# Row normalisation and softmax division moved from VectorE to GpSimd, and the expert product moved one step back in the plan

## What is computed

```
x = x + attn_a(layernorm(x))    # 16 heads of 8, softmax over all keys, mask after the softmax
x = x + ffn(layernorm(x))       # 8 routed experts, top 2 of each row, and one shared expert
x = x + attn_b(layernorm(x))    # rotary q and k, no mask, w_out and a bias behind it
x = x + ffn(layernorm(x))       # the same weights again
layernorm(x) = (x - mean) / sqrt(var + 1e-5)
swiglu(x)    = (silu(x @ w1) * (x @ w3)) @ w2
```

## Time and profile before

| | |
|---|---|
| median of 3 runs | 1904.55 us (1900.91 to 1908.56) |
| the profiled execution | 1906.13 us, its span 1904.1 us |
| mean granted TensorE clock | 0.976 |
| PE busy | 97% |
| DVE busy | 82% |
| ACT busy | 75% |
| POOL busy | 46% |

### The profile page before, as it was taken

One profiled execution on the slowest core, in us unless ns is written; L12 is line 12 of the kernel. 1 busy time (PEld: TensorE's weight loads), 2 busy tenths in 40 slices (PEclk: granted clock), 3 DMA queues, 4 the chain that ended last, 5 costly groups with the idle time before them and its releaser, 6 DMA issues.

```text
span 1904.1 us, 44343 instructions
## 1 busy us (share of the span) xinstructions
PE 1852.5 (97%) x16816; PEld 885.6 (47%) x16816; DVE 1566.8 (82%) x3083; ACT 1432.9 (75%) x2840; POOL 883.0 (46%) x1210
## 2 busy tenths in 40 slices
PE   6999999999999999999999999999999999999997
PEld 3444444444444444444444444444444444444446
DVE  4988998888888888988889888988888888788826
ACT  3388887777777777777788787778877877777782
POOL 6142333455655567555643434435334454544520
PEclk8599998999999999999999999999999999999999
DMA  7111110000100101001100101001100010000000
GB/s 254 35 68 68 58 42 3 1 28 27 52 2 35 35 24 47 2 35 35 35 35 2 51 25 62 2 2 52 40 19 8 2 30 29 24 2 8 7 2 12
DMA packets 39380, 61.91 MB, mean 33 GB/s; under 512 B 5632, under 2 KB 20608, under 8 KB 39040
## 3 DMA queue, kind: packets, MB, share of 16 engines
q1 hardware_dynamic: 39168, 59.08, 9.5%
HBM read 30.74 MB, written 27.26 MB: 30 GB/s over the span
## 4 chain that ended last, share of the span: by engine, by line
PE 86%; DVE 9%; ACT 2%; issue 2%; POOL 1%; DMA 0%; DVEq 0%; ACTq 0%; POOLq 0%
PE ps_sum L1212 28%; PE ps_banks L1178 20%; PE ps_banks L1232 11%; PE ps_banks L1153 9%; PE ps_banks L1253 8%; DVE negmax L940 5%; PE ps_banks L1124 2%; PE ps_banks L1167 2%; PE ps_banks L1131 1%; DVE xn L958 1%; PE ps_banks L1110 1%; PE ps_banks L1223 1%; ACT sums L810 1%; PE ps_banks L1138 1%; PE ps_banks L1160 1%
## 5 line engine op out<-in xcount | busy, mean ns | idle before, releaser
L940 DVE TENSOR_REDUCE negmax<-ps_banks 128x1 f32<-128x512 f32 x2048 | 1280.7, 680 | 196.0 <-PE ps_banks L1153 192.4
L803 ACT ACTIVATE probs<-ps_banks 128x512 f32<-128x512 f32 x2048 | 1085.7, 604 | 195.2 <-PE ps_banks L1178 182.5
L1153 PE MATMUL ps_banks<-kx,qx 24*128 24x512 f32 x2048 | 650.0, 507 | 7.4 <-DVE hid L991 3.6
L1178 PE MATMUL ps_banks<-qx,kx 26*128 26x512 f32 x2048 | 528.6, 500 | 3.5 <-DVE hid L991 1.8
L1212 PE MATMUL ps_sum<-probs,vg 128*9 128x256 f32 (+1 forms) x6144 | 463.8, 374 | 6.8 <-ACT sums L810 6.0
L1178 PEld LDWEIGHTS ps_banks<-qx,kx 26*128 26x128 f32 x2048 | 197.3, 183 | 374.1 <-issue 168.1
L692 POOL TENSOR_SCALAR scaled<-scaled,gates 128x128 f32<-128x128 f32 x516 | 182.9, 372 | 283.1 <-ACT scaled L854 244.2
L1153 PEld LDWEIGHTS ps_banks<-kx,qx 24*128 24x128 f32 x2048 | 260.4, 185 | 103.6 <-ACT probs L803 55.1
L664 POOL TENSOR_TENSOR pdiag<-probs,causal 128x512 f32<-128x512 f32 x128 | 163.5, 1278 | 173.3 <-ACT probs L803 172.4
L680 POOL TENSOR_TENSOR hid<-hid,first 128x512 f32<-128x512 f32 x129 | 164.9, 1278 | 125.8 <-DVE hid L991 121.4
L1212 PE MATMUL ps_sum<-probs,w 128*9 128x256 f32 (+1 forms) x2560 | 187.7, 365 | 2.0 <-ACT sums L810 1.3
(11 more groups left out here) (104 smaller groups left out, 1289.0 us busy)
## 6 DMA issues: line engine op xcount, KB each, us to landing
qk_rows<-limbs SPq DMA_DIRECT2D x36, 512.0 KB, 3.5
qx<-qk_rows SPq DMA_DIRECT2D x128, 96.0 KB
kx<-qk_rows SPq DMA_DIRECT2D x128, 96.0 KB
qx<-mlimbs SPq DMA_DIRECT2D x512, 2.0 KB
qk_rows<-prod_c SPq DMA_DIRECT2D x8, 512.0 KB, 3.7
qk_rows<-prod_s SPq DMA_DIRECT2D x4, 512.0 KB, 2.7
out_dram<-x SPq DMA_DIRECT2D x8, 256.0 KB, 2.3
x<-in_x SPq DMA_DIRECT2D x3, 512.0 KB, 5.9
```

The costliest lines, as they stand in the source:

```text
L803: act.activation(m.probs[:, blk % PROB_SLOTS, EXP_HEADS[k], :], bank, ACT.Exp, scale=SCALE).then_inc(s.freed[SCALAR], 1)
L940: dve.tensor_reduce(m.negmax[:, unit // UNITS % 2, half, col:col + 1], bank, AX.X, ALU.max, negate=True).then_inc(s.freed[VECTOR], 1)
L1153: pe.matmul(bank_of(("scores", unit, k)), m.qx[rows, n % SLOTS, tile * P:(tile + 1) * P], m.kx[rows, n % SLOTS, half * CHUNK:(half + 1) * ...
L1178: pe.matmul(bank, m.kx[rows, n % SLOTS, j * P:(j + 1) * P], m.qx[rows, n % SLOTS, half * CHUNK:(half + 1) * CHUNK], start=True, stop=True) ...
```

## The change

- `apply` runs on POOL. It adds the negated mean and multiplies by the deviation. `deviations` on POOL gets one more small instruction that negates the means (`lower`), and the copy of the means on DVE goes. `apply` stands 3 steps behind `stats` everywhere, where it stood 4 or 5.
- The division is on POOL, in `finish`, together with the addition to x. The reciprocal stays on DVE. Both stand two steps behind `sums`.
- `gated_hidden` runs on DVE at a new item `product`, one step behind `h3`; `hidden` on POOL stays in the step where it was.
- Reads of the ring are counted by a new order, `freed`, in which `h3` counts where `product` stands.
- The expert layers start 2 steps later, and the items behind the second attention 3 steps later.

```
+H3_AT = 3
 def projected_a(c, at):
-    return staged(at, (0, ("stats", 0, c)), (1, ("moments", 0, c)), (4, ("apply", 0, c)), (6, ("turn", 0, c)),
+    return staged(at, (0, ("stats", 0, c)), (1, ("moments", 0, c)), (3, ("apply", 0, c)), (6, ("turn", 0, c)),
...
 def feed_forward(k, at):
-    return staged(at, (0, ("h1", k)), (3, ("h3", k)), (4, ("hidden", k)), (7, ("y", k)), (9, ("gate", k)))
+    return staged(at, (0, ("h1", k)), (H3_AT, ("h3", k)), (H3_AT + 1, ("product", k)), (H3_AT + 1, ("hidden", k)),
+                  (7, ("y", k)), (9, ("gate", k)))
...
-        more, at = routed(1, b * HALVES, HALVES, (b + 1) * HALVES * of_chunk + 11)
+        more, at = routed(1, b * HALVES, HALVES, (b + 1) * HALVES * of_chunk + 13)
...
-        at = (CHUNKS + c + 1) * of_chunk + 9
+        at = (CHUNKS + c + 1) * of_chunk + 12
...
-        add_side(side, {(p + 1) * UNITS + 2 * WEIGH_LAG + 3: [("sums", p)]})
+        add_side(side, staged((p + 1) * UNITS + 2 * WEIGH_LAG + 3, (0, ("sums", p)), (2, ("finish", p))))
...
+        self.read = {SCALAR: {}, VECTOR: {}}
+        for item in plan:
+            held = ("h3", *item[1:]) if item[0] == "product" else item
+            if held[0] in READER and item[0] != "h3":
+                read = self.read[READER[held[0]]]
+                read[held] = len(read)
...
 def deviations(layer, c):
-        pool.wait_ge(s.stats_kept, i + 1)
+        pool.wait_ge(s.stats_done, (i + 1) * CT)
...
+        pool.tensor_scalar(m.lower[:, i % 2, :], m.mv[:, i % 2, :, 0], -1.0, 0.0, ALU.mult, ALU.add
+                           ).then_inc(s.shifted, 1)
...
+    def apply(layer, c):
+        n, i = counts.nth("apply", layer, c), counts.nth("stats", layer, c)
+        pool.wait_ge(s.rstd_done, i + 1)
+        if n >= 2:
+            turned = [item for item in counts.turns if item[0] == "turn"][n - 2]
+            pool.wait_ge(s.filled[SCALAR], counts.use(*turned) + 1)
+        for t in range(CT):
+            tile = c * CT + t
+            last = pool.tensor_scalar(m.xn[:, n % 2, t * P:(t + 1) * P], m.x[:, tile_cols(tile)],
+                                      m.lower[:, i % 2, t:t + 1], m.rstd[:, tile:tile + 1], ALU.add, ALU.mult)
+        last.then_inc(s.xn_done, 1)
...
+    def finish(p):
+        src = m.sums[:, p % 2 * CHUNK:(p % 2 + 1) * CHUNK].rearrange("p (t h r) -> p t h r", t=CT, h=GH)
+        pool.wait_ge(s.inverted, p + 1)
+        pool.tensor_tensor(dst, src[:, :, :, 0:HD], m.recip[:, turn, :, :].to_broadcast([P, CT, GH, HD]), ALU.mult
+                           ).then_inc(s.finished, 1)
+        if masked_after(n):
+            pool.tensor_tensor(cols, cols, dst.rearrange("p t h d -> p t (h d)"), ALU.add).then_inc(s.headed, 1)
...
+    def invert(p):
+        dve.wait_ge(s.freed[SCALAR], counts.freed("sums", p) + 1)
+        if p >= 2:
+            dve.wait_ge(s.finished, p - 1)
+        dve.reciprocal(m.recip[:, turn, :, :], src[:, :, :, HD:HD + 1]).then_inc(s.inverted, 1)
...
-            pe.wait_ge(s.freed[READER[holder[0]]], counts.use(*holder) + 1)
+            pe.wait_ge(s.freed[READER[holder[0]]], counts.freed(*holder) + 1)
```

More of the change, by code:

```diff
@@ L266, in ended @@
     items = [("weigh", blk, part) for blk in range(last - WEIGH_LAG, last) for part in range(2)]
-    items += [("copy", p), ("sums", p)]
+    items += [("copy", p), ("sums", p), ("finish", p)]
     units = list(range(done, 2 * LAYER_UNITS))
@@ L275, in ended @@
         add_side(side, {1 + i * (late - 1) // len(stages): stage})
-    items += [("h1", done), ("h3", done)]
+    items += [("h1", done), ("h3", done), ("product", done)]
     for i, k in enumerate(units):
@@ L279, in ended @@
         if i + 1 < len(units):
-            items += [("h1", k + 1), ("h3", k + 1)]
+            items += [("h1", k + 1), ("h3", k + 1), ("product", k + 1)]
         items.append(("mix", k))
@@ L332, in use, with freed @@
         return self.uses[READER[item[0]]][item]
+    def freed(self, *item):
+        return self.read[READER[item[0]]][item]
     def bank(self, *item):
@@ L629, in low_of_x @@
         t = counts.turns[("turn", layer, c)]
-        pool.wait_ge(s.freed[SCALAR], counts.use("turn", layer, c) + 1)
+        pool.wait_ge(s.freed[SCALAR], counts.freed("turn", layer, c) + 1)
         pool.tensor_tensor(m.x_lo[:, slot, :], m.xt[:, t % 2, :], m.x_hi[:, slot, :].bitcast(F32),
@@ L648, in split_max @@
     def split_max(p):
-        pool.wait_ge(s.freed[SCALAR], counts.use("maxima", p) + 1)
+        pool.wait_ge(s.freed[SCALAR], counts.freed("maxima", p) + 1)
         if p:
@@ L700, in add_scaled @@
         x = m.x[:, chunk_cols(c)]
-        pool.wait_ge(s.freed[SCALAR], counts.use(*item) + 1)
+        pool.wait_ge(s.freed[SCALAR], counts.freed(*item) + 1)
         if i:
@@ L732, in pool_program @@
             mask(*of)
-        elif kind == "sums" and masked_after(place(*of)[0]):
-            add_heads(*of)
+        elif kind == "apply":
+            apply(*of)
+        elif kind == "finish":
+            finish(*of)
         elif kind == "hidden":
@@ L948, in combine @@
                           ).then_inc(s.combined, 1)
[L950 to L958, removed]
-                                     m.mean[:, tile:tile + 1], m.rstd[:, tile:tile + 1], ALU.subtract, ALU.mult)
-        last.then_inc(s.xn_done, 1)
-    def finish(p):
-        n, half = place(p)
-        _, b, g = group_of(n)
+    def invert(p):
         turn = slice(p % 2 * CT, (p % 2 + 1) * CT)
-        dve.wait_ge(s.freed[SCALAR], counts.use("sums", p) + 1)
+        dve.wait_ge(s.freed[SCALAR], counts.freed("sums", p) + 1)
+        if p >= 2:
+            dve.wait_ge(s.finished, p - 1)
         src = m.sums[:, p % 2 * CHUNK:(p % 2 + 1) * CHUNK].rearrange("p (t h r) -> p t h r", t=CT, h=GH)
         dve.reciprocal(m.recip[:, turn, :, :], src[:, :, :, HD:HD + 1]).then_inc(s.inverted, 1)
-        dve.wait_ge(s.inverted, p + 1)
-        if masked_after(n):
-            if p >= 2:
-                dve.wait_ge(s.headed, p - 1)
-            dst = m.heads[:, turn, :, :]
-        else:
-            c = b * HALVES + half
-            if c >= 2:
-                dve.wait_ge(s.filled[SCALAR], counts.use("oturn", c - 2) + 1)
-            dst = m.attn[:, c % 2, :].rearrange("p (t n h d) -> p t n h d", t=CT, n=NG, h=GH)[:, :, g, :, :]
-        dve.tensor_tensor(dst, src[:, :, :, 0:HD], m.recip[:, turn, :, :].to_broadcast([P, CT, GH, HD]), ALU.mult
-                          ).then_inc(s.finished, 1)
     def gated_hidden(k):
@@ L1028, in chain @@
             last = ("logits", layer, c + width - 1)
-            dve.wait_ge(s.freed[SCALAR], counts.use(*last) + 1)
+            dve.wait_ge(s.freed[SCALAR], counts.freed(*last) + 1)
         if k == 2:
@@ L1086, in vector_program @@
             combine(*of)
-        elif kind == "sums":
-            finish(*of)
-        elif kind == "h3":
+        elif kind == "finish":
+            invert(*of)
+        elif kind == "product":
             gated_hidden(*of)
@@ L1121, in queries_keys @@
         t = counts.turns[("turn", layer, c)]
-        pe.wait_ge(s.freed[SCALAR], counts.use("turn", layer, c) + 1)
+        pe.wait_ge(s.freed[SCALAR], counts.freed("turn", layer, c) + 1)
         pe.wait_ge(s.b_weights, DMA * 6)
```

65 lines of the change are left out of this document (31 added, 34 removed).

## The result

The changed kernel takes 2152.06 us (median of 4 runs, 2134.27 to 2158.61) against 1905.66 us for the kernel before on the same chips: 1.128 times as long, 95% interval 1.121 to 1.136. The forecast was 1994 us with a range to 2065. The direction was right and the size was not: 246 us were lost instead of about 90.

A forecast was written before the change was run, and what follows sets the result against it. PE, busy 97%, was taken as the bound. 1904.1 us, +166 for the hold, −55 made up, −25 for DVE's relief and +4 at the start gave 1994 us, range 1918 to 2065.

The forecast's parts named there:

- The bank of `h3`: After `h3`, PE's seventh ring place waits for DVE's product behind two maxima; 126 units, +166 us together.
- Back: −55 us: Part of the hold that PE makes up from 161 us of existing losses; bounds −30 and −124 us.
- the 30 and the 25 us: Old PE losses expected back: 30 us right behind the held place, 25 us as half of the remaining 50.
- Work off DVE: −25 us: 79.8 us of instructions removed from DVE, of which 25 us shorten the kernel; bounds 0 and 80 us.
- Work onto POOL: `apply`, division and negated means take POOL from 883 to 967 us; hidden, 0 us, bound +20 us.
- Rival D: POOL becomes late: `hidden` behind `apply` and `finish` misses `y` in most units; over 2060 us, chance 0.05.
- Start: First transpositions wait for `apply`, now behind both chunks' deviations on POOL; +4 us, bounds 2 and 6.
- B: PE's hold at the bank is mostly made up, since the lost time was due anyway; 1900 to 1960 us, chance 0.15.
- Rival C: DVE is the real bound, so its relief makes the kernel faster; some 1850 us, 1830 to 1895, chance 0.12.
- E: No difference, within 0.5%: PE's modelled times hide a wait already there, the product isn't the last; chance 0.06.

The follow-up runs named there:

- e1: The changed kernel with the product put back in the step of `h3`, ahead of that step's scores; 1913.23 us, ratio 1.000 to the kernel before.
- e2: The kernel before with only the product moved one step behind `h3`, row normalisation and division staying on DVE; 2187.18 us, ratio 1.147.
- e4: The changed kernel with the matmuls of `h3` moved on PE from ahead of their step's exponents to behind its scores; 1927.40 us, ratio 1.010.
- e7: e1 with 8 matmuls of zeros added on PE at 95 places, where no hold stands to fill; 2017.82 us, ratio 1.059.
- e10: e1 with row normalisation on DVE again, so only the division is on POOL, two steps behind the sums; ratio 1.003 to the kernel before.
- e12: The changed kernel with 10 matmuls of zeros on PE in nearly all of the 126 held places; 2084.01 us, ratio 1.096 to the kernel before.
- e5: The changed kernel with the product on DVE between the two score maxima of the step of `h3`; 1974.43 us, ratio 1.036 to the kernel before.
- e9: The changed kernel with the product behind the scores in every second unit only, ahead of them in the others; 2048.89 us, ratio 1.070.

## Why the prediction was right and where it failed

**The bank of `h3`** was right in place, count and length. The step said 126 places, the next scores 2.56 us behind, released by the product. Measured: 126 of 126, 2.53 to 2.54 us in the typical place, PE on 0.055 us after DVE, in 121 of them after standing idle. The sum of +166 us answers to 126 × (2.72 − 1.34) = 174 us. e1, e2 and e4 show that this is the cause.

**"Back: −55 us"** was too generous. The fit puts 0.80 of an added place into the time, so of the 192 us by which the places are longer than in e1 some 39 us come back. Which of the old losses came back, and which of the 30 and the 25 us did not, the runs do not tell apart. e7 shows how little PE can make up: 0.96 us more in each of 126 places, 121 us, became 119 us of span, 18 us of it by the fit because that run had 54 us more at the lower clock.

**"Work off DVE: −25 us"** was too generous too. e1, which has all of it without the hold, is level with the kernel before: from the first exponent to the last its steps take 10.6 us less, and 5.7 us of that are lost at the start. The profile had said it: DVE's wait for scores of 192.4 us meant that saved DVE time would be waited away. DVE's busy time did not fall to 1487 us either but to 1510.0; the maxima alone were busy 1295.5 us, 14.8 us more than before.

**Work onto POOL** was sized well and hidden as said. POOL went to 969.8 us against 967 forecast:

```profile
L648 POOL TENSOR_SCALAR xn<-x,lower,rstd 128x128 f32<-128x128 f32 x128 | 55.4, 444 | 0.7
...
L705 POOL TENSOR_TENSOR heads<-sums,recip 128x128 f32<-128x128 f32 x32 | 13.0, 407 | 58.1 <-DVE recip L989 58.1
```

Normalisation takes 444 ns an instruction where 372 were taken, the division 407 where 455 were. Rival D fell: PE's list of waits has no row for POOL's `hidden` near a microsecond per unit. The measured time lies where D had put it, over 2060 us, but that is chance; its mechanism is absent.

**Start** cost 5.7 us (DVE's first maxima start at 43.13 instead of 37.45 us), within the bounds of 2 to 6 and over the 4 taken. In e10, which has `apply` on DVE, it is gone (36.36 us).

**The step that failed is the sum itself: it had no term for TensorE's clock.** It counted a hold as the time that passes in it, and took every other matmul at its old duration. With PE idle in 121 places for 132.6 us, 310 us more of the span ran at 1.2 GHz; at 0.34 us each that is some 105 us, the larger part of the 163 us between the span forecast, 1994 us, and the one measured. The rest is the 16 us that came back too little, the 14 us too much for DVE's relief, the 2 us more at the start, and the longer places (192 us against e1 where 166 stood in the sum). Put together: 1900.5 + 0.80 × 192 + 0.34 × 310 = 2160 us, measured 2156.8. That the clock's share is real is shown by e12, which keeps the holds and restores the clock, and has a ratio of 1.096 instead of 1.128, some 60 us. That it is 105 us rests on the fit and on the 0.33 between the changed kernel's own executions; by the 0.32 of e12 it would be 99 us.

Rivals B, C and E fell with the 121 waits and with e1. Rival C had a page behind it (the Trainium skill, "Perfetto Trace Analysis", section "Identifying the Most-Contended Engine"), by which the busiest engine of occupancy, DVE with 82%, was to be relieved first, and matmul busy time to be distrusted. Here the measurement decides for the matmul row: 70 us less DVE work changed nothing, and e7's extra matmuls cost nearly their full time, so PE at 97% was the bound. The rule that a two-port VectorE instruction and GpSimd exclude each other (the Trainium skill, "SBUF — State Buffer", section "Who interferes with whom") was not put to a test of its own; the 16 us of DVE time that it offered are inside the relief that bought nothing.

## What to carry to other kernels

Where buffers are handed out in a ring, moving a reader back is not a matter of its own lateness: count the places from its buffer to the one that takes the buffer next, and ask what now stands ahead of the reader on its engine. One step of delay cost 12.8% because it closed a loop of PE and DVE within one step. And when an idle gap is put into a PE that was at 97%, price the gap, then ask what the granted clock will do.

## What the runs showed of the hardware that I had not expected

- Waits of about 1.1 us of idle PE, 121 of them over some 1700 us, came with a mean granted clock of 0.907 where the kernel without them (e1) has 0.976. With PE kept busy by zeros in nearly all of these places it was back at 0.966 (e12). Waits of 0.46 us, 97 of them (e5), left it at 0.965.
- With about half as many of the long waits, 58 (e9), the clock was 0.933, more than half way down. Thinning them out to that number did not spare it; fewer were not run.
- A microsecond at the lower level cost about a third of a microsecond of the whole kernel, and 0.42 us in a typical step with nothing woven in (0.99 us at the upper level, 1.70 at the lower): less than the half that it would be if every duration doubled. That the difference between the two lies in stretches in which PE waits for DVE anyway is only argued.
